# A fused attention and mixture-of-experts layer on one core: the row-maximum pass in 17 pieces over query quarters instead of 18 over query tiles of 128

## What is computed

```python
x = x + attn(layernorm(x))          # 16 heads of dimension 8, causal
    # q, k, v = x @ W.T + b; scores = q k^T / sqrt(8); masked with tril; softmax; @ v; @ Wo.T + bo
x = x + ffn(layernorm(x))           # 8 experts, inner 64, top-1 by argmax of x @ gate_w.T
    # xs = x * sigmoid(top logit) * mask_e;  out += (xs @ w_up.T * silu(xs @ w_gate.T)) @ w_down.T
return x
```

## Time and profile before

| | us |
|---|---|
| median of 3 runs (lowest, highest) | 568.27 (565.29, 571.53) |
| the profiled execution | 567.53 |
| its span in the profile | 565.8 |
| busy in the span: PE, DVE, ACT, POOL | 534.4, 454.1, 379.5, 209.5 |

### The profile page before, as it was taken

The page is one execution under the profiler, slowest core; times in us unless marked ns, Lnnn a source line. Parts: engine busy times, 40 slices in busy tenths (PEclk is TensorE's granted clock), DMA queues, the critical chain, the costliest instruction groups (busy, mean ns, idle before and its releaser), DMA issues.

```text
span 565.8 us, 12240 instructions
## 1 busy us (share of the span) xinstructions
PE 534.4 (94%) x4658; PEld 235.3 (42%) x4658; DVE 454.1 (80%) x669; ACT 379.5 (67%) x770; POOL 209.5 (37%) x393
## 2 busy tenths in 40 slices
PE   4559999999999999999999999999989999999996
PEld 4325433333343332433434334334224455666653
DVE  8847999999999999999999999999923556555631
ACT  1234588898898989889889899898885422222221
POOL 3677364453353443524544346214232111111100
PEclk9879999999999999999999999999997999999999
DMA  6051121420211512102232021120030122111000
GB/s 172 14 154 56 59 63 35 148 56 16 68 30 42 155 32 63 52 21 69 75 107 67 11 65 45 39 69 8 7 101 2 48 57 61 56 57 54 22 19 20
DMA packets 27867, 32.45 MB, mean 57 GB/s; under 512 B 4385, under 2 KB 21281, under 8 KB 27809
## 3 DMA queue, kind: packets, MB, share of 16 engines
q1 hardware_dynamic: 27664, 31.28, 19.4%
q10 hardware_dynamic: 144, 0.39, 0.2%
HBM read 20.26 MB, written 11.01 MB: 55 GB/s over the span
## 4 chain that ended last, share of the span: by engine, by line
PE 69%; DVE 20%; ACT 4%; issue 2%; POOL 2%; DMA 1%; SPq 1%; POOLq 0%; DVEq 0%
PE ps L1058 19%; PE ps L1042 13%; PE ps L999 8%; DVE top_p L823 7%; DVE top_p L821 7%; PE ps L1111 6%; PE ps L1119 5%; PE ps L1108 5%; DVE top_p L816 3%; ACT prob L676 3%; PE ps L1009 3%; PE ps L1109 2%; PE ps L935 2%; PE ps L944 1%; PE ps L1075 1%
## 5 line engine op out<-in xcount | busy, mean ns | idle before, releaser
L676 ACT ACTIVATE prob<-ps 128x512 f32<-128x512 f32 (+2 forms) x640 | 307.8, 561 | 42.7 <-PE ps L1042 37.7
L823 DVE TENSOR_REDUCE top_p<-ps 128x2 f32<-128x1024 f32 x192 | 223.7, 1218 | 4.8 <-PE ps L999 1.2
L1042 PE MATMUL ps<-q_rows,k_rows 51*128 51x512 bf16 (+3 forms) x768 | 169.0, 328 | 2.7 <-ACT prob L676 1.4
L1058 PE MATMUL ps<-prob,v_all 128*9 128x512 f32 (+3 forms) x1536 | 157.8, 492 | 0.5 <-ACT sum_sb L667 0.4
L580 POOL TENSOR_SCALAR_AFFINE_SELECT prob<-prob 128x512 f32<-128x512 f32 x128 | 81.3, 635 | 184.9 <-ACT prob L676 183.1
L999 PE MATMUL ps<-k_rows,q_rows 48*128 48x512 bf16 (+2 forms) x896 | 130.6, 305 | 7.3 <-DMA k_rows<-split_parts 5.0
L1042 PEld LDWEIGHTS ps<-q_rows,k_rows 51*128 51x128 bf16 x768 | 52.3, 93 | 135.5 <-ACT prob L676 120.3
L821 DVE TENSOR_REDUCE top_p<-ps 128x4 f32<-128x1024 f32 x64 | 76.5, 1215 | 0.9 <-PE ps L1009 0.6
L999 PEld LDWEIGHTS ps<-k_rows,q_rows 48*128 48x128 bf16 x896 | 42.6, 94 | 43.8 <-issue 13.3
L719 ACT ACTIVATE prob<-ps 128x512 f32<-128x512 f32 x32 | 19.1, 597 | 56.0 <-PE ps L1109 56.0
L899 DVE TENSOR_TENSOR prob<-ps,prob 128x512 f32<-128x512 f32 x32 | 22.1, 690 | 38.4 <-PE ps L1111 38.4
(11 more groups left out here) (90 smaller groups left out, 420.5 us busy)
## 6 DMA issues: line engine op xcount, KB each, us to landing
split_parts<-part SPq DMA_DIRECT2D x6, 768.0 KB, 5.8
q_rows<-split_parts SPq DMA_DIRECT2D x31, 96.0 KB
k_rows<-split_parts SPq DMA_DIRECT2D x31, 96.0 KB
value_sums<-sum_sb SPq DMA_DIRECT2D x128, 18.0 KB
x_sb<-x SPq DMA_DIRECT2D x8, 256.0 KB, 4.9
qk<-value_sums SPq DMA_DIRECT2D x8, 256.0 KB, 3.7
qk<-inverse_sums SPq DMA_DIRECT2D x8, 256.0 KB, 3.9
out<-y SPq DMA_DIRECT2D x8, 256.0 KB, 2.3
```

The source lines that it names most:

```text
L676: a.activation(prob[:, i % NB, g0:g0 + heads, 0:cols], ps[:, load_at(u, n) % 3, 0:heads * cols].rearrange("p (s t) -> p s t", s=heads), AC ...
L823: return v.tensor_reduce(top_p[:, place, qt, s:s + 3:2], banks, AX.X, ALU.max)
L1042: last = mm(ps[:, l % 3, m * cols:(m + 1) * cols], k_rows[rows, k, s + m, j * P:(j + 1) * P], q_rows[rows, k, s + m, c * HALF + q0:(c + 1) ...
L1058: last = mm(ps[32 * g:32 * g + HD + 1, BANK_V, q0:HALF], v_all[:, b, j, first_head + g, :], prob[:, i % NB, g, 0:n], start=(j == 0), stop= ...
```

## The change

- Query tiles become quarters of 64. The host hands x over with the eight quarters of each 512 tokens in the order 1, 3, 5, 7, 6, 4, 2, 0 and puts the output back. On the chip ACT's `copy_xn` puts the transposed tokens back into natural order with two instructions in place of one, so k and v stay natural; q is projected in the new order with two matmuls of 256 columns in place of one of 512.
- A 128-query tile now pairs a low with a high quarter, and score rows are covered by 17 pieces, five for the first half: one "X" of 64-wide blocks (16 matmuls of 64 columns and one mask matmul a row group over 8 x 64 columns), per half one "Y" of 128-wide blocks (8 matmuls, one mask matmul a row group of 4 x 64) and one "Z" of 128-wide blocks whose two partition halves take different queries and keys (16 matmuls of 128 columns with 64 columns of weights, one mask matmul a row group), two of 256-wide blocks, and 8 of 512 for the second half alone; the 256- and 512-wide ones need no mask. There are 10 mask matmuls a unit in place of 32.
- `join` is two reduces on 64 partitions each, over 64 elements, in place of one on 128 over 32 or 48.
- The turn is one 128 x 48 transpose and a 48 x 128 copy in place of four and a 12 x 512 copy; the send to `q_rows` is in runs of 256 bytes in place of 1 KB.
- In the load and value passes the columns of a slot start 64, 128 or 192 in; widths stay. POOL masks each diagonal slot with two selects of 4 x 64 columns. `send_parts` is two DMAs in place of one.
- `ORDER` is new, 71 letters, and the copy of the previous unit's last sums stands one slot earlier on ACT.

```diff
-SLOTS = [(c, j, max(0, P * j - HALF * c), HALF - max(0, P * j - HALF * c))
+Q = P // 2
+QUARTERS = (1, 3, 5, 7, 6, 4, 2, 0)
+SLOTS = [(c, j, max(0, Q * (j - TPH * c)), HALF - max(0, P * (j - TPH * c)))
          for c in range(2) for j in range(TPH * (c + 1))]
...
+PIECES = [("X", Q, [(c, s, m) for c in range(2) for s in range(2) for m in range(2)], 5)]
+for c in range(2):
+    blocks = [(c, s, m) for s in range(2) for m in range(2)]
+    PIECES += [("Y", P, blocks, 3), ("Z", P, blocks, 4)]
+    PIECES += [("X", 2 * P, [(c, s, 0) for s in range(2)], 6), ("Y", 2 * P, [(c, s, 1) for s in range(2)], 2)]
+    if c == 0:
+        NC0 = len(PIECES)
+PIECES += [(tile, HALF, [(1, s, m)], place) for m in range(2) for tile, place in (("X", 7), ("Y", 1))
+           for s in range(2)]
...
-ORDER = "PSSPVSSVaSSPSSPSVSSPVSPSSSPSVSSPSPSVVSPSSPVSPSSVbSSPSPVSSSPVSPSSPSSSPSVS"
+ORDER = "SPSPSSVVaVSSPPSSVSSSPVSSPSSPSSVSPSPSSVSPSVSPSSPVSSbSPSPSVSPSSVSSPSPSVSS"
...
             def send_parts(b, h, units=range(UPB)):
                 sp.wait_ge(part3_set[h], b + 1)
...
+                for s in range(2):
+                    sp.dma_start(split[:, :, UPB * b + units.start:UPB * b + units.stop, :, :, h, s, :]
...
                         pool.wait_ge(exp_done, slot_loaded(u, i))
-                        blockv = prob[:, i % NB, :, 0:P]
-                        g.affine_select(out=blockv, in_=blockv, pattern=[[0, GH], [1, P]], base=0,
...
+                        for z in range(2):
+                            q0 = (SLOTS[i][3] - Q) * z
+                            quarter = prob[:, i % NB, :, q0:q0 + Q]
+                            last = g.affine_select(out=quarter, in_=quarter, pattern=[[0, GH], [1, Q]],
...
-                        if i == 1 and u:
+                        if i == 0 and u:
                             take_sums(u - 1, 1)
...
             def join(u, c):
...
+                for h in range(2):
+                    rows = slice(Q * h, Q * h + Q)
+                    last = v.tensor_reduce(top[rows, c].rearrange("p g (k m) -> p k g m", k=2),
+                                           top_p[rows, c, h:h + 8].rearrange("p (k z) g m -> p k g m z", k=2),
+                                           AX.X, ALU.max)
...
             def piece(u, n, r):
...
+                for y, (c, s, m) in enumerate(blocks):
                     for rg in range(2):
...
+                        if tile == "Z":
+                            for h in range(2):
+                                q0 = (2 + m) * P if h == 0 else m * P + Q
+                                k0 = (1 - m) * 2 * P + Q if h == 0 else m * 2 * P + P
+                                last = mm(ps[Q * h:Q * h + Q, first_bank + rg, cols],
+                                          q_rows[rows, k, c, s, q0:q0 + Q], k_rows[rows, k, c, s, k0:k0 + P],
+                                          start=(y == 0), stop=False, skip_group_check=True)
+                            continue
...
+                if masked:
+                    for rg in range(2):
...
+                        last = mm(dst, pick[rows, PICK[tile]:PICK[tile] + P],
+                                  shade[rows, None, :].to_broadcast((64, len(blocks), Q)),
+                                  start=False, stop=True, skip_group_check=True)
                 return last
```

More of the change, by code:

```diff
@@ L25 @@
 ROWS_M = ROWS + 3
+TOP_COLS = 2 * 3 * 2 * TPH
 INV_COLS = HEADS * SEQ // P
@@ L332, in send_parts @@
                 sp.wait_ge(part3_set[h], b + 1)
[L333 to L338, removed]
+                for s in range(2):
+                    sp.dma_start(split[:, :, UPB * b + units.start:UPB * b + units.stop, :, :, h, s, :]
+                                 .rearrange("e n u d r t -> (u d r) (e n) t"),
+                                 part[64 * s + 16 * units.start:64 * s + 16 * units.stop, h, :, :, :]
+                                 .rearrange("p e n t -> p (e n) t")).then_inc(split_out[h], 16)
             def load_rows(u):
@@ L481, in _ @@
             for rg in range(2):
[L482 to L489, removed]
+                rows = slice(Q * rg, Q * rg + Q)
+                both = pick[rows, Q:3 * Q].rearrange("p (h t) -> p h t", h=2)
+                chain.link(g.affine_select(out=both, in_=both, pattern=[[0, 2], [-1, Q]], base=0,
+                                           channel_multiplier=1, compare_op=ALU.not_equal, fill=1.0))
+                chain.link(g.affine_select(out=shade[rows, :], in_=shade[rows, :], pattern=[[-1, Q]], base=0,
+                                           channel_multiplier=1, compare_op=ALU.is_ge, fill=MASKED))
             g.memset(v_all[:, :, :, :, HD:HD + 1], 1.0).then_inc(v_ones_set, 1)
@@ L1003, in piece @@
-                if masked[0]:
-                    for e in range(2):
-                        for rg in range(2):
-                            rows = slice(64 * rg, 64 * rg + 64)
-                            dst = (ps[:, first_bank + rg, :].rearrange("p (m t) -> p m t", t=width)
-                                   [:, :, width - P + 64 * e:width])
-                            last = mm(dst, pick[rows, e, :],
-                                      shade[rows, e, None, 64 * e:P].to_broadcast((64, len(blocks), P - 64 * e)),
-                                      start=False, stop=True, skip_group_check=True)
+                        cols = slice(y * width, (y + 1) * width)
@@ L1196 @@
     r = run_bass_kernel_spmd(nc, [given], core_ids=[0])
-    return r.results[0]["out"]
+    return by_quarter(r.results[0]["out"], [QUARTERS.index(n) for n in range(len(QUARTERS))])
```

151 lines of the change are left out of this document (77 added, 74 removed).

## The result

The changed kernel takes 576.49 us (574.53 to 578.94, 4 runs) against 569.9 (565.29 to 571.98, 4 runs): a ratio of 1.0127, with a 95% interval of 1.008 to 1.0174. The prediction was 557 us, faster. The profiled execution took 574.93 us, its span is 572.7 against 565.8.

What follows compares the result with a forecast made beforehand. DVE was taken as nearly the bound, with PE also near its limit. Units falling from 22.75 to 22.0 us save 11.3 over 15, the rest 0: 567.5 becomes 556.2, stated as 557 us, range 548 to 565.

Steps and rivals of the forecast that it cites:

- the sends in runs of 256 bytes ... nothing: Sends to `q_rows`: some 5 us from turn to first load of the second half, so shorter runs cost nothing.
- the 0.3 us for `send_parts`: Lead-in: one more DMA issue on SP before the first rows come back, 0.3 us (0 to 1.1).
- a unit is 20.7 + 0.8 + 0.35, and 0.15 for places where the others come last: Ordinary unit: DVE's work, its idle time, extra idling at the unit's start, and an allowance for PE and ACT: 22.0 us.
- the 0.6 taken: Joins on DVE: about 0.25 us a unit before, 0.35 more (0.2 to 0.65) with four longer ones.
- gap before Z: Start of the unit: DVE idles 0.65 to 0.9 us between the turn's copy and the Z reduce.
- 0.10 at each end of Z: PE: changing the kind of matmul into and out of each Z costs 0.10 us each time.
- slower: Rival: matmuls with 64 columns of weights run one at a time; unit about 23.3 us, total 576; chance 0.08.
- PE takes over: Rival: PE at 21.2 us or more governs the unit, which takes 22.45; total 563.8; chance 0.15.
- The change doesn't do what it says: Rival: DVE was not the bound, ACT's handshake sets the time; unit 22.6 us, total 566; chance 0.07.
- As tight as the old one: Rival: the new order has no costlier unit start; unit 21.5 or 21.2 us, total 549 to 545; chance 0.2.
- The second select on POOL: Diagonal slots: POOL takes 0.80 us for 0.635, hidden because values come three slots later; cost nothing.
- three terms of 0.9, 0.6 and 0.3 us: Lead-in: one piece less gains 0.9 us; two-instruction `copy_xn` costs 0.6 and the extra `send_parts` issue 0.3; together 0.

Runs made afterwards that it cites:

- x1_parts_early: Changed kernel with the four DMAs of the next sequence's parts issued before the second half's maxima: 568.1 us against 569.47 before, ratio 0.9952.
- x2_before_split: Kernel before, with the parts of sequences 1 to 3 sent in two DMAs of 64 partitions per half, not one of 128: 575.7 us.
- x4: Changed kernel with the letter b, the turn of the next unit's first half, 11 letters earlier: 585.85 us.
- x3_join_one: x1_parts_early with each join as one reduce over 128 partitions, not two over 64, leaving out part of the joining: 563.78 us.
- x5: x1_parts_early with the letters of the kernel before, less the P at their head, and the sums copied a slot later: 572.04 us.
- x6_new_deal: x1_parts_early with other letters, and the sums' copy placed as in the kernel before: 563.27 us against 570.03, ratio 0.9881.
- x7_no_masks: x1_parts_early without the 10 mask matmuls of a unit in the pass for the maxima: 564.83 us.
- x9_half_keys: x1_parts_early with the 16 matmuls of the eight 512-wide pieces covering 256 keys, not 512: 564.47 us.
- x10: x1_parts_early with both the joins as one reduce each and no mask matmuls in the pass for the maxima: 564.21 us.
- x8_one_select: x1_parts_early with one of POOL's two selects on each diagonal slot left out: 561.43 us.

## Why the prediction was wrong

The sum was 556.2 on the profiled execution's scale, and that execution took 574.93: 18.7 us to explain. Term by term:

- *Three waits for the maxima, 5.4 us (1.83 + 1.83 + 1.74).* The step that failed is "the sends in runs of 256 bytes ... nothing", together with the 0.3 us for `send_parts`. I priced the second DMA only at the start of the kernel and looked for the maxima's slack from the turn on. I never asked what SP's program has in front of them. x1_parts_early keeps the runs of 256 bytes and has no wait, so the runs were rightly priced; it is SP's 4.68 us for the parts that were not. x2_before_split shows it from the other side.
- *The clock after two of the waits, 3.3 us (1.59 + 1.68).* Not in the sum. That the waits bring it about is likely, not shown. It goes with them in x1_parts_early, and x2_before_split has one just behind its third wait. But of the nine such waits of the changed kernel, x2 and x4 only three were followed by a fall, and x4 has two falls away from its waits.
- *The fall in the first unit, 2.4 us.* Not in the sum, and its cause stays open. x1, x3, x5, x6, x7, x9 and x10 have one between 67.8 and 76.2 us, with first units of 23.2 to 24.6; the kernel before, x2, x4 and x8 have none, with 22.5 to 23.5. x8 differs from x1 by work of POOL alone, so the new letters don't force it.
- *The ordinary unit, 22.49 for 22.0, 7.4 us in 15.* The step was "a unit is 20.7 + 0.8 + 0.35, and 0.15 for places where the others come last": DVE's work plus its gaps. The terms in it were partly wrong (joins 1.1 us in all for the 0.6 taken, Z's own matmuls 0.25 for 0.36) and partly right (pieces 1.15 for 1.16, copy 0.21 for 0.22, gap before Z 0.66 for 0.65 to 0.9, 0.10 at each end of Z). DVE's work came out at 21.08 for 20.7, by the joins, and its idle time at 1.41 for 1.3: in the terms of the sum that is 0.38 and 0.11 of the 0.49. But the joins' price can't be what is wrong alone: x3_join_one has DVE at 20.6, and the unit is 22.37, because the idle time grows to 1.8. The form of the sum, work plus fixed gaps, is what failed. With DVE busy for 94% of the unit, ACT for 88% and PE by the prediction's own sum for 92%, a cut on one engine becomes its idle time. x3 passed on a quarter of the cut, x9 a quarter, x7 nothing, while moving letters changed the unit from 22.17 to 23.45 with the same work.

These terms make 18.5 of 18.7.

Of the rivals, *slower* named 576 us, but by Z matmuls that run one by one, and Z takes 0.35 us to its mask: the number was met by another mechanism. *PE takes over* gave 22.45 for the unit. The chain of the ordinary unit does give PE the larger part (61%), but x7_no_masks took 0.66 us from PE without effect and x9_half_keys 0.88 for 0.21, so it isn't PE's work alone either. *The change doesn't do what it says* gave 22.6 by ACT's handshake, 0.11 from the measured 22.49; since no run takes work from ACT, it isn't excluded. *As tight as the old one* needed 21.5; x6_new_deal, with a better order than the changed kernel's, reaches 22.17.

The rule of the Trainium skill (TensorEngine Tiling (Array Packing), Key Properties) that a change of tiling mode drains the engine would have put 0.2 us on each Z. The trace agrees: from a load in 64-row tiles into Z's 64 by 64 tiles there are 0.09 us more, and from Z to its mask 0.10 more, than between steps in tiles of one kind. It shows the time and not that a drain is what takes it. That tiles run in parallel is borne out too: Z's matmuls start in fours, and four such groups take 0.25 us, the 0.24 of full overlap and not the 0.48 of none.

The second select on POOL was rightly costed at nothing, as x8_one_select shows. For the lead-in three terms of 0.9, 0.6 and 0.3 us cancelled in the sum, and for the last unit and the second stage nothing was put. 67.70 against 67.80 us to the first exponential and 156.5 against 156.9 from the last unit's agree with that, but no run measures the terms one by one, and the clock stood at 1.2 GHz in these stretches for different times, so the close agreement is partly luck.

## What to carry to other kernels

When a step is split into more DMAs, go through the program of the queue that issues them and look at what stands behind them, in every unit in which they occur; here 3.7 us more of issuing in three units cost 8.7 us with the clock, where the 15 faster units gave 3.8. Where three engines are all near 90% and run one fixed interleaving, as here, work taken off one of them may give little (here a quarter or less) until the interleaving is dealt anew for it, and an edit's price can't be read from one engine's sum. Look for a lower granted clock behind a late DMA: here it followed three of nine waits, and cost 1.3 to 1.7 us each time.

## What the runs showed of the hardware

- The issue of a 384 KB DMA of 1 KB pieces on SP took 0.6 to 1.7 us each in four, 4.68 together, where two of 768 KB took 0.98 together (in x2_before_split the four took 4.96). The loads issued just behind the four took 1.56 and 1.35 us, and behind the two 1.14 and 1.39, in place of the 0.65 of later ones.
- A reduce of 64 partitions over 64 elements in four dimensions takes 0.26 us, and two of them don't overlap, while the next piece began 0.11 us behind the start of a join of 128 partitions over 32 elements, and 0.24 behind one over 48.
- Sixteen matmuls of 128 columns in 64 by 64 tiles start in fours and take 0.25 us, with 0.09 us more on entering from 64-row tiles and 0.10 on leaving.
- A granted clock of 1.2 GHz for 3.4 us cost a unit 1.0 to 1.7 us (eight cases), for 6.8 us 0.9 to 2.4 (five cases).
